# Three products of a constant matrix with itself ahead of two waits of TensorE in the routing stage of a vision-transformer block

## The reference, cut to what matters

```
logits = xf @ w_router + b_router                  # xf: the normalised tokens, 1184 x 256, 8 experts
topv, topi = top_k(softmax(logits), 2)
onehot = one_hot(topi.reshape(-1), 8)
pos = cumsum(onehot, axis=0)[arange(2n), e_flat] - 1     # the place of each choice in its expert
keep = pos < cap                                         # cap = int(1.25 * n / 8) = 185
buf = zeros(8, cap, d).at[e_flat, min(pos, cap-1)].add(keep * xf[tok])
h = gelu(einsum(buf, w1) + b1); out = einsum(h, w2) + b2
y[token] = sum over its kept choices of weight * out / sum of its kept weights
```

## Time and profile before

| | us |
|---|---|
| median of 3 runs | 174.18 |
| lowest, highest | 172.84, 174.77 |
| the profiled execution's own time | 173.59 |
| its span | 171.8 |
| TensorE's mean granted clock over the span | 0.97 of full speed |

### The profile page before, as it was taken

The page is one execution under the profiler, slowest core; times in us unless marked ns, Lnnn a source line. Parts: engine busy times, 40 slices in busy tenths (PEclk is TensorE's granted clock), DMA queues, the critical chain, the costliest instruction groups (busy, mean ns, idle before and its releaser), DMA issues.

```text
span 171.8 us, 2880 instructions
## 1 busy us (share of the span) xinstructions
PE 158.7 (92%) x1029; PEld 148.6 (87%) x1029; DVE 68.6 (40%) x276; ACT 60.4 (35%) x148; POOL 49.8 (29%) x51
## 2 busy tenths in 40 slices
PE   7899999999999699989899999999999999999910
PEld 7479999986885699889799999999999999999900
DVE  0085873597689995978420301102002020030010
ACT  4116552426445039433035062250521605306010
POOL 2005322044040000004408338074370642406041
PEclk9999999999999858999999999999999999999995
DMA  5999920093031502500488877789767897502213
GB/s 186 409 408 423 382 79 0 20 384 130 4 106 53 159 6 70 161 18 27 95 293 199 300 248 164 224 219 296 241 147 228 235 279 237 83 0 27 23 8 37
DMA packets 17151, 28.37 MB, mean 165 GB/s; under 512 B 1273, under 2 KB 13763, under 8 KB 17013
## 3 DMA queue, kind: packets, MB, share of 16 engines
q1 hardware_dynamic: 14677, 25.38, 43.7%
q0 software_dynamic: 2464, 2.86, 9.7%
HBM read 24.10 MB, written 4.14 MB: 164 GB/s over the span
## 4 chain that ended last, share of the span: by engine, by line
PE 73%; DVE 14%; DMA 6%; issue 2%; POOL 2%; POOLq 1%; SPq 0%; ACT 0%; ACTq 0%; DVEq 0%
PE ps L1128 22%; PE ps L1118 21%; PE ps L1024 6%; PE ps L978 6%; PE ps L1039 4%; DMA first_t<-first 4%; PE ps L959 3%; DVE prod L755 2%; DVE z_s L753 2%; PE ps L1136 2%; DMA rows_in<-xrows,src_row 2%; DVE onehot L730 2%; PE ps L1106 1%; DVE at_p L895 1%; PE ps L943 1%
## 5 line engine op out<-in xcount | busy, mean ns | idle before, releaser
L584 ACT ACTIVATE hid<-ps,b_cur 128x186 f32<-128x186 f32 x64 | 23.1, 412 | 57.9 <-PE ps L1118 57.9
L463 POOL DMA_INDIRECT out_rows<-out_s,dst_row x16 | 23.7, 1483 | 47.8 <-ACT out_s L595 39.4
L868 DVE COPY buf_t<-ps 128x372 f32<-128x372 f32 (+1 forms) x8 | 4.2, 520 | 47.7 <-PE ps L1106 47.6
L448 POOL DMA_INDIRECT rows_in<-xrows,src_row x14 | 13.9, 991 | 32.0 <-DVE src_row L846 28.0
L1118 PE MATMUL ps<-buf_t,w_even 128*128 128x186 f32 x128 | 21.7, 321 | 0.7 <-DVE buf_t L868 0.7
L1128 PE MATMUL ps<-hid,w_even 128*128 128x186 f32 x128 | 21.7, 321 | 0.0
L1118 PE MATMUL ps<-buf_t,patch_t 128*128 128x186 f32 x128 | 21.5, 320 | 0.0
L1128 PE MATMUL ps<-hid,patch_t 128*128 128x186 f32 x128 | 21.5, 321 | 0.0
L1118 PEld LDWEIGHTS ps<-buf_t,w_even 128*128 128x128 f32 x128 | 20.2, 190 | 1.0 <-issue 1.0
L1128 PEld LDWEIGHTS ps<-hid,patch_t 128*128 128x128 f32 x128 | 20.3, 190 | 0.0
L1128 PEld LDWEIGHTS ps<-hid,w_even 128*128 128x128 f32 x128 | 20.3, 190 | 0.0
(11 more groups left out here) (159 smaller groups left out, 223.1 us busy)
## 6 DMA issues: line engine op xcount, KB each, us to landing
w_even<-w SPq DMA_DIRECT2D x8, 1024.0 KB, 5.5
patch_t<-w SPq DMA_DIRECT2D x8, 1024.0 KB, 5.3
patch_t<-patches SPq DMA_DIRECT2D x2, 972.0 KB, 12.0
att<-attn SPq DMA_DIRECT2D x1, 1280.0 KB, 9.2
first_t<-first SPq DMA_DIRECT2D x1, 870.0 KB, 6.8
xrows<-xn SPq DMA_DIRECT2D x3, 288.0 KB, 2.4
out_rows<-h SPq DMA_DIRECT2D x3, 288.0 KB
first_t<-first SPq DMA_DIRECT2D x1, 580.0 KB, 4.1
```

What stands on the lines that cost most here:

```text
L448: pool.indirect_dma_start(out=rows_in[q][0:SIZES[s], s, :], out_offset=None, in_=xrows[:, :], in_offset=bass.IndirectOffsetOnAxis(ap=src_r ...
L463: pool.indirect_dma_start(out=out[:, :], out_offset=bass.IndirectOffsetOnAxis(ap=dst_row[0:SIZES[s], c:c + 1], axis=0), in_=out_s[q][0:SIZ ...
L584: ins = act.activation(hid[:, f, :], bank(pair)[:, (f % 2) * SL:(f % 2 + 1) * SL], ACT.Gelu, bias=b1_cur[q][:, f:f + 1])
```

## The change

A helper `bridge()` issues three products of `mean_mat` with itself into columns 512 to 639 of the slot of unit `("a", C)`. That slot's second bank is in use by no unit between `bridge()` and `("norm2", E)`, which comes behind both calls. It is called ahead of `claim` of two units, `("norm2", C)` and `("slots", 0)`. Nothing is taken away, no wait is added, and no other engine's program changes.

```diff
 KEEP_WARM = 3
+BRIDGE = 3
...
+            def bridge():
+
+                spare = slot("a", C)[:, 512:640]
+                for _ in range(BRIDGE):
+                    pe.matmul(spare, mean_mat[:, :], mean_mat[:, :], start=True, stop=True)
+
             for u, (kind, n, _slot) in enumerate(UNITS):
+                if (kind, n) in (("norm2", C), ("slots", 0)):
+                    bridge()
                 claim(u)
```

## The result

The changed kernel took 172.07 us in the median of 15 executions (171.32 to 174.96), the kernel before 174.0 us (172.8 to 174.86, also 15). The ratio is 0.988 with a 95% interval of 0.985 to 0.991, which is 1.2% faster; between the medians lie 1.9 us, or 1.1%. The forecast was 173.1 us and 0.6%, in a range of 172.1 to 174.5 us. The direction was right, the size was half of the measured one, and the time lies just under the low end of the range. The case that came about is the first rival, in which the clock does not fall; it was given a chance of 0.30 and a time of 172.5 us.

The account below looks back on a forecast made before the run. TensorE was taken to bound the kernel, with one clock dip near 60 us. From the profiled 173.59 us the path gains 0 to 0.45 us with a later fall; 173.1 us was taken as median, range 172.1 to 174.5 us.

Parts of the forecast that it names:

- the first rival: The clock does not fall at all, since the filled stretch up to 59.3 has no hole; 172.5 us, chance 0.30.
- What bounds the kernel, and what the dip costs: VectorE sets the time until 62.26, then `pick(0)` on TensorE, which lost 1.77 us at half rate.
- The term: Without the dip, `place` 1 would start at 67.54 instead of 68.66, 1.12 us earlier, limited by `chosen` of the second half.
- The time without a fall: The floor: the profiled 173.59 us less 1.12 us, which is 172.5 us.
- The costs of the bridges: Ahead of `norm2` C and `slots` 0: 0.84 us per three products, covered; bounds 0 and +0.15 us on the path, taken as 0.
- The price at the lower level: Read from the warm-up: 2.93 us for six products, 1.46 us for three, 0.49 us for one.
- What stands between 59.3 and 62.26 is not covered: From `slots` 0 to `pick(0)`, light work plus 1.2 us idle would make the clock fall between 61 and 63.5 us.
- The first bridge: Three products ahead of `norm2` C fill a TensorE wait of 0.82 us and help keep the clock up until 59.3.
- Idle time as the measure: From 55.6 to 59.3 TensorE has no idle time over 0.15 us, so the fall at 58.96 goes in most executions.
- The scatter: The runs of before scatter over 1.9 us, read as the same dip falling and rising at other points of the work.
- the short fall that I had forecast: The clock falls later and rises 3 to 4 us after, over `pick(0)`; 173.1 to 173.6 us, chance 0.46.
- The slower rival: The lower level keeps its 6.84 us and moves onto `pick(0)`; 175.1 us, chance 0.09 together with other losses.

Follow-up runs that it names:

- late_three: Against the kernel before: three products behind `slots` 0 and no other bridge; 172.7 us, clock up in 2 of 4 executions.
- third_again: Against the kernel before: neither bridge, four products ahead of `pick(0)`, measured a second time; 172.26 us, clock up in 1 of 9.

## Why the prediction was right or wrong

*What bounds the kernel, and what the dip costs.* Right. VectorE sets the time up to `pick(0)`, TensorE on it; `chosen` of the second half caps the gain. The term was 1.12 us in the forecast and 1.27 us in the profiles. The time without a fall, 172.5 us, was still too high by 0.4 us against the profiled 172.06 us: the rest is mostly the 0.17 us by which this execution was ahead from the start, and which the sum held fixed at the value of one execution.

*The costs of the bridges.* Right at 0, with a price per product that was a quarter too high. The price at the lower level, 0.49 us, came from the warm-up, where the clock column reads 1.00, so those rows do not show which level it is; `late_three` gives 1.42 us for three at 0.50, or 0.47 us each.

*"What stands between 59.3 and 62.26 is not covered ... between 59.3 and 62.26 there is a stretch of the kind that made the clock fall."* This is the step that failed. The stretch is there as described, with 1.39 us of idle time at its end, and the clock stays up through it in 16 of 21 executions (by the mean clock; in both profiles the column reads 1.00). So light work with a hole of that length was not enough here to bring the clock down in most executions, once three products of 128 columns stood just ahead of it. I compared the stretch that is left with a part of the one that had fallen, the 3.5 us from `y` E to `slots` 0, and found them alike. But in the kernel before the light work does not end at `slots` 0: it runs on from the end of `y` E to `pick(0)`, 6.5 us without one wide product of the kind that the bridges add (its transposes are as wide), and in the second profile the clock falls only 5.4 us into it. What the second bridge leaves on either side is less than half of that.

The length of the light work is not the whole cause either. In the profiles of `late_three` and `third_again`, whose program on TensorE is that of the kernel before up to there, the clock fell at 57.9 and 57.7, some 2.2 us behind the end of `y` E, and the second bridge leaves more than that on both sides. And products at the edges are not alike: three or six next to `y` left the median where it was, four next to `pick(0)` won 1.6 us. What decides in which execution the clock falls, and where, stays open; shown is that three wide products ahead of `slots` 0 kept it up in most (7 of 10 by themselves, 16 of 21 with the first bridge).

*The first bridge.* I gave both the same share in keeping the clock up. It has none that can be measured (7 of 10 executions with the clock up without it, 16 of 21 with it). The hole of 0.82 us that it fills lies next to the dense work of `y`; that this is the reason is likely, not shown.

*Idle time as the measure.* The forecast counted "no idle time over 0.15 us" as the reason why the fall at 58.96 would go. The narrow products close the second of the two holes, and the clock falls; the wide ones close no more than that, and it mostly stays up. The better count was the wide products, of which the text has the number too ("1.7 us of it in products of 128 columns"), but beside the wrong one.

*What the light work is made of.* `norm2` E, transposes and router products together, stood in the light stretch in all kernels. The clock read 1.00 through it in both profiles of the changed kernel and 0.50 in the first of before. No run parted the transposes from the narrow products, so the fall can't be put down to either.

*The scatter.* Read in part rightly as the same dip at other points of the work, and the second profile of before shows it. But differences of up to 0.9 us arise in the first projection, long before the dip (the last section has the rows), and the sum did not have them: where the short fall that I had forecast came about, with the second bridge alone, the execution took 172.41 us and not 173.1 to 173.6, and it was already 1.0 us ahead of the first profile of before at `y` E (53.90 against 54.91). I also took the profiled execution (173.59 us) as typical. Ten of the kernel's 15 executions are slower, and the 0.4 us between it and the median of 174.0 are why the gain of the medians, 1.9 us, is larger than the 1.5 us between the two profiled executions.

*The slower rival.* Two of 15 executions of the changed kernel have its time (174.93 and 174.96 us, against 175.1) and a mean clock of 0.964 and 0.965, so it may have taken place in them; neither was profiled. They are as slow as the slowest executions of before (174.86 us), hardly slower.

## What to carry to other kernels

When a clock dips behind light work, look at the whole run of light work, at the full clock, up to the next dense group, and ask for more than one execution before pricing it; between the two profiles of the kernel before the fall moved from 58.96 to 61.0 us, and `pick(0)` took 5.78 and 6.88 us. Products that are to hold the clock did so here from the middle of such a run, and when they were wide (clock up in 7 of 10, 171.53 and 171.69 us); idle time that was filled at its early edge (0 of 10, 174.35 us), or with narrow products (0 of 10, 173.72 us), bought nothing, and wide ones at its late edge bought most of the time (2 of 19, 172.23 and 172.26 us). So try the places one at a time. A wait of TensorE for another engine is the free place for such products, as long as what follows has the cover, here 0.55 us.

## What the runs showed of the hardware that was not expected

TensorE's clock fell from 1.00 to 0.50 while the engine was recorded busy without a gap: with the narrow products it was busy for the whole microsecond from 58, and the clock was 0.78 in it and 0.50 in the next. It also stayed at 1.00 through 1.39 us of idle time with 1.6 us of light work ahead of it, in the changed kernel.

The stays at the lower level in the middle of the kernel were not of any length. In the ten profiled executions that have one it lasted 3.4 us in two, 6.8 us in seven and 10.2 us in one, and it began anywhere from 57.7 to 62.4 us.

The step between two products (clock up in 2 of 10, over 172.5 us in 7) and three (7 of 10, and none) is large for a difference of 0.22 us of work.

Profiled executions also differ by about 0.9 us from the start, where the programs are still the same. The first 24 instructions of the first projection take 8.19 us in the profiled execution of the changed kernel and 7.24 us in that of the second bridge alone:

```profile
3.73 8.19 PE L1048 MATMUL ps<-first_t 128*128 128x324 f32 x24
```
```profile
3.74 7.24 PE L1048 MATMUL ps<-first_t 128*128 128x324 f32 x24
```

Most of the difference is still there at `y` E (54.73 and 53.90). With the clock up, the executions of the changed kernel spread from 171.2 to 172.4 us, and this may be the reason, though its two profiles agree (8.19 and 8.23 us). In the first profile of the kernel before, the same projection stood still in its middle for its input:

```profile
8.47 3.54 PE L1039 MATMUL ps<-first_t 128*128 128x324 f32 x12 [0.62 <-DMA first_t<-first]
```

What makes the projection longer in the others was not measured.
